# Rotation of the queries and keys moved from VectorE to ScalarE and GpSimd, attention divisions moved to GpSimd, and the hand-written orders and banks laid anew

## What is computed

```python
x = x + _L0_xcond_ref(ctx, _layernorm(x), ...)      # 16 heads of 64, keys: context and x
x = x + _L0_ffn_ref(_layernorm(x), ...)             # ternary weights, 8-bit activations
x = x + _L1_xcond_ref(_layernorm(x), ...)           # six layers
x = x + _L1_ffn_ref(_layernorm(x), ...)             # eight experts
```

```python
xn = _adaln(x, noise_emb, n1_w[i], n1_b[i])
q = _rope(q.reshape(B, L, H, HD)); k = _rope(k.reshape(B, L, H, HD))   # H = 16, HD = 8
x = x + _attn(q, k, v, src_mask).reshape(B, L, D) @ so_w[i].T
q = _rope((xn @ cq_w[i].T).reshape(B, L, H, HD))                      # xn: second norm of x
k = _rope((context @ ck_w[i].T).reshape(B, LC, H, HD))
x = x + _attn(q, k, v, ctx_mask).reshape(B, L, D) @ co_w[i].T
x = x + gelu(_adaln(x, ...) @ f1_w[i].T + f1_b[i]) @ f2_w[i].T + f2_b[i]
```

## Time and profile before

| | |
|---|---|
| median of 3 runs | 2330.6 us (2330.3 to 2330.8) |
| the profiled execution's own time | 2330.7 us |
| its span | 2328.9 us |
| mean granted TensorE clock | 0.970 of full speed |
| share of the span, busy | PE 93%, DVE 86%, ACT 73%, POOL 47% |
| mean busy share of the 16 DMA engines, by slice of the span | mostly 0.1 to 0.2 in the 24 steps |

### The profile page before, as it was taken

The page is one execution under the profiler, slowest core; times in us unless marked ns, Lnnn a source line. Parts: engine busy times, 40 slices in busy tenths (PEclk is TensorE's granted clock), DMA queues, the critical chain, the costliest instruction groups (busy, mean ns, idle before and its releaser), DMA issues.

```text
span 2328.9 us, 44949 instructions
## 1 busy us (share of the span) xinstructions
PE 2174.1 (93%) x16458; PEld 887.6 (38%) x16458; DVE 1996.2 (86%) x4031; ACT 1701.3 (73%) x3457; POOL 1088.9 (47%) x1348
## 2 busy tenths in 40 slices
PE   6999999999678999999999999999999999999879
PEld 3445455545422233333333333333333333333336
DVE  6778889698789989999999999999999999988435
ACT  4778868688156778787888787787877888777534
POOL 3556657466443344544444444544444445442223
PEclk9999999999679999999999999999999999999869
DMA  2000000000412222212222222222122222221000
GB/s 85 2 1 1 2 1 2 31 1 2 108 47 59 60 78 62 62 49 77 61 74 64 56 76 66 68 62 80 49 62 57 84 63 67 57 60 38 24 21 19
DMA packets 108564, 112.98 MB, mean 49 GB/s; under 512 B 15809, under 2 KB 96951, under 8 KB 107319
## 3 DMA queue, kind: packets, MB, share of 16 engines
q1 hardware_dynamic: 108345, 110.12, 17.1%
HBM read 14.80 MB, written 1.05 MB: 7 GB/s over the span
## 4 chain that ended last, share of the span: by engine, by line
PE 51%; DVE 28%; ACT 9%; issue 4%; POOL 3%; DMA 3%; SPq 2%; DVEq 0%; POOLq 0%; ACTq 0%
DVE A L2059 12%; PE psum L1578 7%; PE psum L1558 5%; PE psum L1546 4%; PE psum L1666 4%; PE psum L1638 4%; PE psum L1479 3%; PE psum L1433 3%; DVE A L2091 3%; ACT A L2301 3%; PE psum L1658 3%; ACT A L2239 3%; DVE A L2135 2%; PE psum L1445 2%; PE psum L1536 2%
## 5 line engine op out<-in xcount | busy, mean ns | idle before, releaser
L2301 ACT ACTIVATE A<-psum 128x512 f32<-128x512 f32 x1536 | 828.1, 599 | 253.6 <-PE psum L1546 237.2
L2059 DVE TENSOR_REDUCE A<-psum 128x1 f32<-128x512 f32 x1536 | 957.9, 679 | 43.2 <-PE psum L1558 41.4
L1558 PE MATMUL psum<-A 64*128 64x512 bf16 x1536 | 448.3, 390 | 30.4 <-issue 12.5
L1546 PE MATMUL psum<-A 64*128 64x512 bf16 x1536 | 422.1, 385 | 23.1 <-ACT A L2301 10.6
L1578 PE MATMUL psum<-A 128*9 128x512 f32 (+1 forms) x3072 | 408.7, 605 | 4.0 <-ACT A L2301 2.0
L2428 POOL TENSOR_TENSOR A<-A,rden 128x512 f32<-128x512 f32 x256 | 266.8, 1068 | 177.4 <-DVE rden L1933 176.7
L2321 ACT ACTIVATE A<-psum 77x512 f32<-77x512 f32 x384 | 219.8, 595 | 45.4 <-PE psum L1627 39.7
L1558 PEld LDWEIGHTS psum<-A 64*128 64x128 bf16 x1536 | 110.4, 94 | 313.8 <-ACT A L2301 88.8
L2447 POOL TENSOR_SCALAR A<-A 128x4 f32<-128x4 f32 x72 | 16.4, 228 | 425.6 <-DVE A L2049 425.3
L1546 PEld LDWEIGHTS psum<-A 64*128 64x128 bf16 x1536 | 101.4, 95 | 290.5 <-ACT A L2301 120.2
L2239 ACT ACTIVATE A<-psum,nm 128x512 f32<-128x512 f32 x256 | 176.2, 688 | 44.9 <-DVE nm L1921 44.0
(11 more groups left out here) (207 smaller groups left out, 3706.3 us busy)
## 6 DMA issues: line engine op xcount, KB each, us to landing
A<-A SPq DMA_DIRECT2D x456, 128.0 KB, 2.4
A<-A SPq DMA_DIRECT2D x336, 64.0 KB, 2.0
A<-zero SPq DMA_DIRECT2D x51, 128.0 KB, 2.3
wl<-in_wl SPq DMA_DIRECT2D x6, 1024.0 KB, 5.8
A<-A SPq DMA_DIRECT2D x36, 78.0 KB, 2.1
A<-in_nT SPq DMA_DIRECT2D x1, 1664.0 KB, 7.2
A<-in_w SPq DMA_DIRECT2D x2, 512.0 KB, 6.8
A<-in_w SPq DMA_DIRECT2D x1, 1024.0 KB, 6.0
```

The source lines that it names most:

```text
L1546: handle.matmul(bank(b), k_st[bt][lo:lo + ROW, h // 2, k * P:(k + 1) * P], q_st[m % 3][lo:lo + ROW, h // 2, :], start=True, stop=True).the ...
L1558: handle.matmul(bank(b), q_st[m % 3][lo:lo + ROW, pair, q * P:(q + 1) * P], k_st[bt][lo:lo + ROW, pair, :], start=True, stop=True).then_in ...
L2059: handle.tensor_reduce(nm[:, pair // 4, q, j, pair % 4:pair % 4 + 1], bank(BANKS["maximum"][i]), AX.X, ALU.max, negate=True).then_inc(mx, 1)
L2301: handle.activation(pT[:, block % 2, i % GROUP, :], bank(BANKS["scores"][i]), ACT.Exp, scale=HD1 ** -0.5).then_inc(ex, 1)
```

## The change

- **Rotation.** ScalarE copies the projection as it is from PSUM into `unswapped` (new parts qk_raw twice, cq_raw, and ck_raw once a layer). The swap moves these raw rows. GpSimd makes both products: raw by cosine into `t1`, and, after the swap has landed, `t2` by sine in place; then it adds and cuts into thirds as before. VectorE's qk_rope, cq_rope and ck_rope are gone. The sine table is laid out on the host for rows already swapped.
- **Divisions.** o_divide and co_divide are run by GpSimd, with two semaphores each (o_rd and o_dv, co_rd and co_dv) between o_invert, the division and o_back.
- **Late rows.** `other_rows` is cut in two parts, other_zeros and other_rows; both stand in the queue where the whole stood, before the first shift rows, one right behind the other.
- **Orders and banks.** All five tables, the PLACED_ tables and BANKS are new. VectorE's list has 86 parts a step where it had 96, ScalarE's 93 (89), GpSimd's 13 (11), TensorE's 191 as before. In GpSimd's list f_bias now stands between f_norm and c_thirds. In SyncE's list the key swap stands ahead of the query swap, but in step 0 the query's rows go out before the keys' swap.

The diff, cut to the parts named here (of the tables only a few places are shown):

```diff
         TENSOR = {
-                        "cq": 798,
-                        "co": 997,
...
-                        "cross_max": [857, 863, 865, 871, 875, 876, 881, 883],
...
+                        "co": 1067,
...
+                        "cq": 884,
...
+                        "cross_max": [923, 925, 926, 930, 936, 944, 947, 952],
         }
         POOL = {
-                        "c_thirds": 55,
-                        "f_bias": 67,
-                        "shift": [35, 40],
-                        "s_norm": 25,
-                        "cshift": 59,
-                        "q_thirds": 27,
-                        "k_thirds": 28,
-                        "c_norm": 52,
-                        "ck_thirds": 42,
-                        "f_norm": 65,
+                        "k_thirds": 39,
+                        "q_thirds": 40,
+                        "shift": [48, 54],
+                        "c_norm": 68,
+                        "co_divide": 82,
+                        "ck_thirds": 57,
+                        "f_norm": 84,
+                        "f_bias": 85,
+                        "c_thirds": 73,
+                        "s_norm": 36,
+                        "cshift": 76,
+                        "o_divide": 64,
...
@@ -1230,6 +1196,9 @@
                 zeros(A_Q + A_STACK, A_K, MASK_SLOT, S)
                 zeros(A_CQ, A_V, MASK_SLOT, 284)
                 zeros(A_CK, A_V, SHIFT_SLOT, B * CP)
+
+            def other_rows():
+
                 sp.wait_ge(zeroed, 8 * 16)
                 stack_rows((A_Q + A_STACK, A_K), (A_K + A_STACK, A_CQ), range(1, B), zeroed)
                 ones(A_CQ, A_CK, slice(MASK_SLOT, P, ROW), S, zeroed)
...
@@ -2029,11 +2000,6 @@
 
                 return handle.reciprocal(rd, of_heads(o)[:, :, :, HD1])
 
-            def divide(o, rd):
-
-                rows = of_heads(o)[:, :, :, 0:HD1]
-                return handle.tensor_tensor(rows, rows, rd.unsqueeze(3).to_broadcast([P, S // 32, 2 * HALVES, HD1]), ALU.mult)
-
             def flip_back(o, attT):
 
...
-                    invert(o_s, rd_s).then_inc(own.next(), 1)
-                if name == "o_divide":
-                    after_own()
-                    divide(o_s, rd_s).then_inc(own.next(), 1)
+                    invert(o_s, rd_s).then_inc(o_rd, 1)
                 if name == "o_back":
-                    after_own()
+                    dve.wait_ge(o_dv, m + 1)
                     dve.wait_ge(so_ps, m)
                     flip_back(o_s, attT_s).then_inc(att, 1)
...
@@ -2119,31 +2073,6 @@
...
-                if name == "qk_rope":
-                    turned = (tq, tk)[i // 2]
-                    dve.wait_ge((sp_q, sp_k)[i // 2], 3 * m)
-                    if i >= 2:
-                        dve.wait_ge(sp_ck, 3 * min((m + 2) // B, NL))
-                        dve.wait_ge(f_yT, m - 3)
-                    if i == 0:
-                        dve.wait_ge(q_rows, 112 * m)
-                    if i == 2:
-                        dve.wait_ge(k_rows, 96 * m)
-                        dve.wait_ge(ck_rows, 96 * min((m + 2) // B, NL))
-                    dve.wait_ge(in_late, 96)
-                    dve.wait_ge(qk_ps, 2 * m + i // 2 + 1)
-                    handle.tensor_tensor((turned.unswapped, turned.t1)[i % 2], bank(BANKS["qk"][i // 2]), (sinT, cosT)[i % 2][:, :], ALU.mult).then_inc(qk_ro, 1)
-                if name == "ck_rope" and bt == 0:
...
+                if name == "qk_raw":
+                    act.wait_ge((sp_q, sp_k)[i], 3 * m)
+                    if i == 0:
+                        act.wait_ge(q_rows, 112 * m)
+                    else:
+                        act.wait_ge(sp_ck, 3 * min((m + 2) // B, NL))
+                        act.wait_ge(k_rows, 96 * m)
+                        act.wait_ge(ck_rows, 96 * min((m + 2) // B, NL))
+                    act.wait_ge(qk_ps, 2 * m + i + 1)
+                    handle.activation((tq, tk)[i].unswapped, bank(BANKS["qk"][i]), ACT.Copy).then_inc(qk_ro, 1)
+                if name == "cq_raw":
+                    act.wait_ge(sp_c, 3 * m)
+                    act.wait_ge(c_rows, 112 * m)
+                    act.wait_ge(cq_ps, m + 1)
+                    handle.activation(tcq.unswapped, bank(one("cq")), ACT.Copy).then_inc(cq_ro, 1)
+                if name == "ck_raw" and bt == 0:
+                    act.wait_ge(sp_k, 3 * min(m + 2, STEPS))
+                    act.wait_ge(k_rows, 96 * min(m + 2, STEPS))
+                    act.wait_ge(ck_rows, 96 * l)
+                    act.wait_ge(ck_ps, l + 1)
+                    handle.activation(tk.unswapped[:, 0:B * CP], psum[:, one("ck"), 0:B * CP], ACT.Copy).then_inc(ck_ro, 1)
                 if name == "f_mod":
                     act.wait_ge(f_yT, m + 1)
                     act.wait_ge(f1_ps, 4 * m)
...
+            def by_keys(t, table):
+
+                if t.shape[1] == S:
+                    return t, table[:, :]
+                return t.rearrange("p (b c) -> p b c", b=B), table[:, 0:CP].unsqueeze(1).to_broadcast([P, B, CP])
+
             def thirds(w, n, ready_sem, ready, swapped, spare, done_sem, base):
+                pool.wait_ge(in_late, 96)
                 pool.wait_ge(ready_sem, ready)
+                t1, t2, raw, hi, mid, lo = (t[:, 0:n] for t in (w.t1, w.t2, w.unswapped, w.hi, w.mid, w.lo))
+                (a1, cos), (a2, sin), (a0, _) = by_keys(t1, cosT), by_keys(t2, sinT), by_keys(raw, cosT)
+                handle.tensor_tensor(a1, a0, cos, ALU.mult).then_inc(own.next(), 1)
                 pool.wait_ge(*swapped)
-                t1, t2, hi, mid, lo = (t[:, 0:n] for t in (w.t1, w.t2, w.hi, w.mid, w.lo))
+                handle.tensor_tensor(a2, a2, sin, ALU.mult).then_inc(own.next(), 1)
+                after_own()
                 handle.tensor_tensor(t1, t1, t2, ALU.add).then_inc(own.next(), 1)
                 for s, value in spare:
...
+            def of_heads(o):
+
+                return o[:, :, 0:2 * HW * HALVES].rearrange("p b (x d) -> p b x d", d=HW)
+
+            def divide(o, rd):
+
+                rows = of_heads(o)[:, :, :, 0:HD1]
+                return handle.tensor_tensor(rows, rows, rd.unsqueeze(3).to_broadcast([P, S // 32, 2 * HALVES, HD1]), ALU.mult)
+
             def shift_thirds(src, rem, third):
                 handle.tensor_copy(third(0), src).then_inc(own.next(), 1)
...
                 if name == "c_thirds":
-                    thirds(tcq, S, cq_ro, 2 * m + 2, (c_swap, 64 * (m + 1)), ((c_rows, 112 * m), (csh_rows, 16 * m)), sp_c, 3 * m)
+                    thirds(tcq, S, cq_ro, m + 1, (c_swap, 64 * (m + 1)), ((c_rows, 112 * m), (csh_rows, 16 * m)), sp_c, 3 * m)
+                if name == "o_divide":
+                    pool.wait_ge(o_rd, m + 1)
+                    divide(o_s, rd_s).then_inc(o_dv, 1)
+                if name == "co_divide":
+                    pool.wait_ge(co_rd, m + 1)
+                    divide(o_c, rd_c).then_inc(co_dv, 1)
                 if name == "cshift":
...
                 if name == "q_thirds":
-                    thirds(tq, S, qk_ro, 4 * m + 2, (q_swap, 64 * (m + 1)), ((q_rows, 112 * m),), sp_q, 3 * m)
+                    thirds(tq, S, qk_ro, 2 * m + 1, (q_swap, 64 * (m + 1)), ((q_rows, 112 * m),), sp_q, 3 * m)
                 if name == "k_thirds":
-                    thirds(tk, S, qk_ro, 4 * m + 4, (k_swap, 64 * (m + 1 + min((m + 2) // B, NL))), ((k_rows, 96 * m), (ck_rows, 96 * min((m + 2) // B, NL))), sp_k, 3 * m)
+                    pool.wait_ge(f_yT, m - 3)
+                    thirds(tk, S, qk_ro, 2 * m + 2, (k_swap, 64 * (m + 1 + min((m + 2) // B, NL))), ((k_rows, 96 * m), (ck_rows, 96 * min((m + 2) // B, NL))), sp_k, 3 * m)
...
         "cosT": cosT,
-        "sinT": sinT,
+        "sinT": c(sinT.reshape(2, 2, 32, S)[:, ::-1].reshape(P, S)),
         "mask": twice(words(g["mask_BxS_bf0"])),
         "maskc": twice(words(padded(g["mask_BxS2_bf0"]))),
```

1195 lines of the change are left out of this document (572 added, 623 removed), and 8 rows, old and new, of the table PLACED_POOL.

## The result

The changed kernel takes 2351.1 us (median of four runs, 2348.2 to 2352.2) against 2330.5 (2328.9 to 2330.8): ratio 1.0082, 95% interval 1.0068 to 1.0096. I had 2292 with a range of 2250 to 2335. The profiled execution took 2352.2 us, its span is 2350.3. Every median here is of runs in the fast state, so one slow run of e10 (3919.7 us) and two of before are left out.

What follows compares the result with a forecast made beforehand. PE (floor 60.4 us) and DVE (59.9) nearly fill the 63.65 us step; DVE relieved gives 61.8. From 2330.7 us, 23 steps × 1.85 take 42.6, start 0, end +4: 2292.1, range 2250 to 2335.

Steps and rivals of the forecast that it cites:

- PE's floor: PE's summed work without waits: 60.4 us of the 63.65 us step, the same before and after the change.
- Contention: VectorE's divisions, with two full SBUF inputs, contend with GpSimd; they average 1.08 us, from 0.68 to 1.54.
- The cross path: From the start of cq to the first cross maximum: 16.45 us against PE's 16.0, about half a microsecond late.
- o_back's wait: o_back on DVE waits for POOL's division: hidden behind maxima if POOL is free, otherwise some 1.3 us of DVE each.
- the sentence on queries and keys: Next queries' and keys' rotations on POOL: at most 17.8 us of some 24, leaving 6 for copy, swap and rows.
- my signs: Trace signs of right or wrong, such as PE's chain share up (right) or first cross maximum released by DMA (wrong).
- the same floor: PE's small matmuls in the new list cost 20.8 us a step, as in the old list.
- DVE's relief: Rotation and divisions off DVE take 6.3 us a step, from 59.9 to 53.6.
- The start: First maxima and rows before the steady steps: between a gain and a loss of 4.4 us, taken as 0.
- The end: Last two steps, where nothing covers a rotation: second products and two uncovered divisions cost +4 us.
- No gain: Rival: a closed round of hand-overs sets 63.65 us and moves with the lists; 2331 plus 0 to 4; chance 0.10.
- Slower: Rival: cross path late at f_norm and c_thirds, which wait for x_co; step 64.8 us, time 2361; chance 0.16.

Runs made afterwards that it cites:

- e10: Changed kernel with the cross query's rotation back on VectorE, new lists and banks kept: 2351.0 us, ratio 1.0088.
- e11: Changed kernel with the rotations of queries, keys and cross query back on VectorE, divisions on GpSimd, new lists kept: 2369.5 us, ratio 1.0167.
- e6: Kernel before with only its two divisions moved to GpSimd; rotation, lists and banks as before: 2341.0 us, ratio 1.0046.
- e2: Changed kernel with both GpSimd products of every rotation left out: 2304.0 us, ratio 0.9881.
- e14: Changed kernel with the products of the queries', keys' and context keys' rotations left out: 2315.5 us, ratio 0.9941.
- e13: Changed kernel with the two products of the cross query's rotation left out: 2335.3 us, ratio 1.0023.
- e7: Kernel before with the new rotation alone; divisions on VectorE, old lists and banks but a few places: 2485.9 us, ratio 1.0670.
- e8: Kernel before with the new rotation and divisions on GpSimd, old lists and banks but a few places: 2502.1 us, ratio 1.0741.
- e4: Changed kernel with c_zero ahead of c_rows in SyncE's queue: 2336.1 us, ratio 1.0031.
- e16: Kernel before with its two divisions on GpSimd only in steps 4 to 19: 2321.3 us, ratio 0.9967.

## Why the prediction was wrong

The runs make a chain from before to after in which each link changes one part, with the limits of e11 said above (spans of the profiled executions; steady step in brackets):

```
before                                 2328.9  (63.93)
e6   divisions to GpSimd                +10.2  (-0.42)
e11  the new lists, same work           +30.0  (+1.29)
e2   rotation off VectorE, free         -71.9  (-2.65)
after  its products on GpSimd           +53.1  (+1.87)
after                                  2350.3  (64.02)
```

By medians the links are +10.5, +28.5, −65.5 and +47.1 us: the profiled execution of e2 was the fastest of its four, that of the changed kernel the slowest. By spans I forecast −38.6 us and got +21.4. Of these 60 us, 31 lie between steps 4 and 20, 12 in the first four steps and 18 at the end.

**Right.** *PE's floor and what relief of DVE brings.* I had 61.8 us a step; with the products free (e2) it is 62.15, near it; the floor of 60.4 itself no run reached. *Prices*: products 1.27, divisions 1.08, copies 0.60, POOL 39.1 us of a step (39.0). The Trainium skill (GPSIMD Engine Reference, 4.1 Engine selection) puts GpSimd at about twice VectorE's time for two inputs; the traces agree, 1.27 against 0.68 for the products. *Contention*: DVE's divisions took 676 to 1539 ns; on POOL all 48 take 1.07 to 1.09 (last section). *The cross path*: 16.1 us measured, 16.45 said, but in part by luck. I charged 2.4 us for f_bias and a product; both had ended at 1410.23, just before the swap landed, so they cost nothing there, and c_zero's landing, which I left out, is what came last. *o_back's wait* isn't on the chain.

**Wrong, the step that failed.** "POOL goes from 29.3 to 39.0 of 63.65, which as a load costs nothing", with the sentence on queries and keys: at most 17.8 us of 24, "which leaves 6 for copy, swap and rows", priced at zero. In the round shown the two copies take 2.2 us, SyncE's issues 1.9, the key's swap 3.2 to land (2.0 in most rounds), the rows 2.5: that is 9.8, not 6. POOL's part was 14.3, not 17.8, since one product lies beside the swap and the casts take 0.62, not 1.27. The sum is 24.1, and 22.8 to 23.2 in most rounds, for a window that I put at 24 and that is 22.4. A path that fills its window to the last microsecond is no cover, it is a bound, and e14 prices its products: 1.09 us a step and all 9 us before step 0. I worked out the cross path to 0.05 us and took half a microsecond of lateness to be all there was. I added its loss to a step in which the other path was held to be early, but the two lie in series in one round (e13 + e14 = e2). Together their products cost 1.87 us a step, as much as the whole gain that I forecast (1.85). Two of my signs say the same: PE's share of the chain was to rise and fell from 51% to 35%, and the first cross maximum released by a DMA, a sign of being wrong, came (L1581, 0.7 us a step).

**Wrong, the lists.** I found "the same floor" for the new lists and charged them nothing. At the same work they are up to 1.29 us a step worse (e11 against e6), 30 us in all, of which about half is the place that I gave the products; they are what this rotation needs (e7, e8). How much of it the changed kernel itself pays, no run separates.

**Wrong, a term taken too large.** DVE's relief: 55.3 us, not 53.6. Between steps 4 and 20 the divisions off DVE free 1.6 us a step (before to e6) for the 2.2 that I took off, and the rotation 3.2 (e11 to e2) for 4.1. The durations overlap in the record, which explains part of it: e11's products last 0.67 but start 0.60 apart.

**The start**: 0 ± 4.4 was right in sum (−1.2), by luck. By the table the divisions cost 4.6 there (e6) and the products 8.6 (e2), while the new lists, with the condition matmuls ahead, give 8.6 (e11 against e6) and the rotation off DVE 5.8 (e2 against e11). The first four steps lost 5.0 where I had a gain; e6 loses 5.1 there with the divisions alone. **The end**: I had +4 and it is +16.2. e6 shows 6.2 of it with the divisions alone, e2 shows 8.2 for the products, for which I had 2.4.

**The rivals.** *No gain* (0.10) had the mechanism, a closed round of hand-overs, but not its member POOL. Between steps 4 and 20 it came nearest (+0.09 us a step); in time *slower* did, 2361 against 2351. *Slower* (0.16) named the wrong place: x_co follows co's move (x_co at 1402.20, cq at 1403.96), and f_norm is through before the swap has landed. What is late is the chain behind the copies. c_zero behind c_rows, an edit that I named in no term, costs 15 us (e4).

## What to carry to other kernels

Moving work to an idle engine is priced by the path through that engine, not by its load: write the path out from the first producer to the consumer, with every queue and landing, and compare it with the window. If it fills the window, it is the new bound, and two such paths in one round add up. Price an edit of the order at something, above all where two short transfers change places in one queue. And a change of work between engines in a kernel with fixed lists can be used in part: only in the steps where it gains (e16).
